# The last item's normalisation in the attention stage and in the scan stage, moved from GpSimd to ScalarE and VectorE

## The chip, the cores and the metric

The kernel runs on one core of a Trainium2 chip. The time is the device time of one launch in microseconds. A core has TensorE (matmuls, PE in the rows, PEld its weight loads), VectorE (DVE), ScalarE (ACT), GpSimd (POOL) and SyncE (SP), which here only asks for DMAs. Each engine runs a program of its own; they meet by semaphores.

## What is computed

Four layers of an attention part and a feed-forward part over x of 2048 rows of 256 numbers (8 items of 256 rows). The reference ends so, and each of the eight lines is a stage of the kernel:

```python
def _layernorm(x, axis=-1, eps=1e-05):
    m = jnp.mean(x, axis=axis, keepdims=True)
    v = jnp.var(x, axis=axis, keepdims=True)
    return (x - m) / jnp.sqrt(v + eps)
...
    x = _layernorm(x + _L1_attn_ref(x, ...), axis=-1)   # attention stage, l1_attn
    x = _layernorm(x + _L1_ffn_ref(x, ...), axis=-1)    # expert stage, l1_ffn
    x = _layernorm(x + _L2_attn_ref(x, ...), axis=-1)   # scan stage, l2_attn
    x = _layernorm(x + _L2_ffn_ref(x, ...), axis=-1)    # ternary stage, l2_ffn
```

The attention stage has 16 heads of 128. The expert stage routes each row to 4 of 32 experts. The scan stage is a selective scan with 16 states for each of 512 channels. The change concerns the last step of the attention stage and of the scan stage: for the last item, mean and variance of a row are known, and (x - m) / sqrt(v + eps) has to be written back.

## The kernel before

`program` (L4000) runs the stages one after the other. Each stage is a function that opens a `Block` in which it writes a program for each engine, and after it an `all_engine_barrier` (L4065) clears the stage's semaphores. X, the 8 items of x (128 rows x 2 x 256 each), stays in SBUF over all stages and is overwritten item by item.

At the end of a `Block` every engine executes a DRAIN, reports on a semaphore, and waits; GpSimd gathers the reports and releases the others. The barrier on L4065 does so a second time, with GpSimd clearing the semaphores between. The records of the first are put down to the line of the stage's `ExitStack`: L977 for the attention stage, L1444 for the expert stage, L1899 for the scan stage, L2586 for the ternary stage. A stage's first instructions follow the second.

The end of a stage for item i is made by helpers that all stages share. `add_and_stats` and `mean_and_variance` (L132 to L150): VectorE adds the residual into `r`, takes statistics of both halves of 128 rows, and aggregates them into `mv` (mean, variance), which raises `var_ready` by 1 for each half. `rstd` (L153): GpSimd waits for `var_ready`, adds `eps` into `vpe`, and takes it to the power of -0.5 into `rstd`. `normalize` (L161): VectorE waits for `rstd_ready` and writes X by a subtraction and a product for each half.

```python
def rstd(ph, pool, i):
    pool.wait_ge(ph.var_ready, (i + 1) * NT)
    ph.nc.gpsimd.tensor_tensor(ph.vpe[:, :], ph.mv[:, :, 1], ph.eps[:, :], ALU.add).then_inc(ph.eps_added, 1)
    pool.wait_ge(ph.eps_added, i + 1)
    ph.nc.gpsimd.tensor_tensor(ph.rstd[:, :], ph.vpe[:, :], ph.half[:, :], ALU.pow).then_inc(ph.rstd_ready, 1)
```

**Attention stage** (`l1_attn`, L968). The loop runs over 8 items and within them over 16 heads in a software pipeline of seven steps; the residual and the normalisation of item i - 1 stand inside item i. Beside it the kernel already routes the rows for the expert stage: GpSimd scatters the normalised rows of items 0 to 5 to memory, by indirect DMAs of 128 rows each, 8 for each item (`scatter`, L1404), two items late. After the last head VectorE takes the last item's residual and statistics, GpSimd its root (L1114), VectorE normalises (L1399), and nothing is left to overlap them with. SyncE asks for the experts' weights as the heads' weights are no longer needed, the last pieces when the last head's products are made.

**Expert stage** (`l1_ffn`, L1431). It begins with the transposes and the routing of the last item, the scatter of items 6 and 7, and the loads of sorted rows. GpSimd also asks here for the ternary stage's raw weights and stores them quantised (L1569, L1578).

**Scan stage** (`l2_attn`, L1878). GpSimd gathers the experts' results by 64 indirect DMAs (L2007), the last in item 4. In each item 16 scans run on VectorE; GpSimd multiplies each result by C (L2064), TensorE sums over the states. The normalisation is made another way here: GpSimd computes the root and also -mean * rstd (`pool_norm`, L2012, four operations, by `pool_rstd_out` for the stage's end), and ScalarE writes X with it as bias and scale (`act_out`, L2358). For the last item these stand at the end of GpSimd's and ScalarE's programs (L2084, L2441), behind the output product of the last item.

**Ternary stage** (`l2_ffn`, L2576). It loads its weights from memory after the barrier, turns them on TensorE, and then runs dense matmuls.

Of the kernel before, what the change touches and what calls it, by code (L numbers as in the profile page):

```python
# [20 lines left out]
ACT = mybir.ActivationFunctionType  # L21
AX_X = mybir.AxisListType.X

ITEMS, SEQ, D = 8, 256, 256
NT = SEQ // P
# [42 lines left out]
class Steps:  # L68
# [15 lines left out]
    def end(self):  # L84
        assert self.n == self.per_item, self.n
# [7 lines left out]
def stage(ph, pool, i):  # L93

    pool.wait_ge(ph.x_turned, i)
    ph.nc.gpsimd.tensor_copy(ph.xin[:, :, :], ph.X[:, i]).then_inc(ph.x_staged, 1)
# [56 lines left out]
def rstd(ph, pool, i):  # L153

    pool.wait_ge(ph.var_ready, (i + 1) * NT)
    ph.nc.gpsimd.tensor_tensor(ph.vpe[:, :], ph.mv[:, :, 1], ph.eps[:, :], ALU.add).then_inc(ph.eps_added, 1)  # L156
    pool.wait_ge(ph.eps_added, i + 1)
    ph.nc.gpsimd.tensor_tensor(ph.rstd[:, :], ph.vpe[:, :], ph.half[:, :], ALU.pow).then_inc(ph.rstd_ready, 1)


def normalize(ph, dve, i):  # L161

    dve.wait_ge(ph.rstd_ready, i + 1)
    for j in range(NT):
        ph.nc.vector.tensor_scalar(ph.X[:, i, j], ph.r[:, j, :], ph.mv[:, j, 0:1], ph.rstd[:, j:j + 1],  # L165
                                   ALU.subtract, ALU.mult).then_inc(ph.x_done, 1)
# [801 lines left out]
def l1_attn(nc, sh, w):  # L968
# [8 lines left out]
    with ExitStack() as ctx:  # L977
        ph = Phase(nc, ctx, "l1a", sh)
# [50 lines left out]
        def run(item, end):  # L1029

            def of(engine):
                item(0, 0, range(NH), first=True)
                item(1, 1, range(NH), second=True)
                for i in range(2, ITEMS):
                    item(i, i % 2, range(NH))
                end()
            return of
# [36 lines left out]
        @block.gpsimd  # L1074
        def _(pool):
            nc.gpsimd.memset(ones32[:, :], 1.0).then_inc(ones_ready, 1)
            pool.wait_ge(ones_ready, 1)
            nc.gpsimd.tensor_copy(ones[:, :], ones32[:, :]).then_inc(ones_ready, 1)
            stage(ph, pool, 0)
            nc.gpsimd.memset(routes.ones[:, :], 1.0).then_inc(consts_cleared, 1)  # L1080
            nc.gpsimd.memset(routes.lc[:, :, routes.E:], BIG).then_inc(consts_cleared, 1)
            nc.gpsimd.memset(routes.sel[:, :, :], 0.0).then_inc(consts_cleared, 1)
            nc.gpsimd.memset(routes.run[:, :, :], 0.0).then_inc(consts_cleared, 1)
            nc.gpsimd.memset(routes.base[:, :], 0.0).then_inc(consts_cleared, 1)
            nc.gpsimd.iota(room[:, :], [[routes.ROOM, routes.E]], base=0, channel_multiplier=0,
                           allow_small_or_imprecise_dtypes=True).then_inc(consts_cleared, 1)
            nc.gpsimd.memset(routes.ones_e[:, :], 1.0).then_inc(consts_cleared, 1)
            nc.gpsimd.iota(routes.full[:, :], [[P, ITEMS * NT]], base=P - 1, channel_multiplier=0,
                           allow_small_or_imprecise_dtypes=True).then_inc(consts_cleared, 1)
            nc.gpsimd.iota(routes.tau[:, :], [[0, 1]], base=0, channel_multiplier=1,  # L1090
                           allow_small_or_imprecise_dtypes=True).then_inc(consts_cleared, 1)
            pool.wait_ge(consts_cleared, 9)

            nc.gpsimd.affine_select(out=routes.tri[:, :], in_=routes.ones[:, :], compare_op=ALU.is_gt, fill=0.0,
                                    base=0, pattern=[[1, P]], channel_multiplier=-1).then_inc(consts_ready, 1)
            nc.gpsimd.tensor_copy(routes.base[0:1, :], room[0:1, :]).then_inc(consts_ready, 1)
            pool.wait_ge(consts_ready, 2)
            nc.gpsimd.memset(routes.base[32:33, :], 1.0).then_inc(consts_ready, 1)
            pool.wait_ge(consts_ready, 3)
            stage(ph, pool, 1)  # L1100
            for i in range(1, ITEMS):
                stage(ph, pool, i + 1)
                rstd(ph, pool, i - 1)
                pool.wait_ge(ph.x_done, i * NT)
                if i > 1:
                    pool.wait_ge(routing.turned, i - 1)
                nc.gpsimd.tensor_copy(xr, ph.X[:, i - 1]).then_inc(routing.x_ready, 1)
                if i == 2:
                    pool.wait_ge(sh.rows_cleared, 16)
                if i >= 2:  # L1110
                    pool.wait_ge(routing.idx_ready, i - 1)
                    for j in range(NT):
                        scatter(nc, pool, sh, i - 2, j, qk_ready, i * NH + 9 + j * routes.TOPK)
            rstd(ph, pool, ITEMS - 1)  # L1114

        @block.tensor
        def _(pe):
# [84 lines left out]
        def _(act):  # L1202
# [52 lines left out]
                        keep_high(ph, act, i + 1, xh[1 - p], YB[1 - p])  # L1255

            run(item, lambda: item(ITEMS - 1, 1, range(NH, NH + 6)))(act)

        @block.vector
        def _(dve):  # L1260
            keep_low(ph, dve, 0, xh[0], xl[0], xl_ready, YB[0])

            def residual(k, q):
                dve.wait_ge(ph.y_ready, k + 1)
                add_and_stats(ph, dve, k, YB[q][:, :].rearrange("p (j n) -> p j n", j=NT))
# [130 lines left out]
            def end():  # L1396
                item(ITEMS - 1, 1, range(NH, NH + 6))
                residual(ITEMS - 1, 1)
                normalize(ph, dve, ITEMS - 1)  # L1399

            run(item, end)(dve)

# [1 line left out]
def scatter(nc, pool, sh, i, j, pace=None, begun=0):  # L1404

    routes = sh.routes
    landed = routes.rows_out if i < ITEMS - 2 else routes.late_rows_out
    for k in range(routes.TOPK):
        if pace is not None:
            pool.wait_ge(pace, begun + k)  # L1410
        nc.gpsimd.indirect_dma_start(  # L1411
            out=sh.moe_rows, out_offset=bass.IndirectOffsetOnAxis(ap=routes.idx[:, i * NT + j, k:k + 1], axis=0),
            in_=sh.X[:, i, j, :], in_offset=None).then_inc(landed, 16)
# [464 lines left out]
def l2_attn(nc, sh, w):  # L1878
# [20 lines left out]
    with ExitStack() as ctx:  # L1899
        ph = Phase(nc, ctx, "l2a", sh)  # L1900
# [125 lines left out]
        def pool_rstd_out(pool, k):  # L2026
            pool_norm(pool, k, ph.var_ready, ph.eps_added, ph.rstd_ready, ph.x_done, shift_ready, ph.mv, ph.vpe, ph.rstd, r_sh)
# [6 lines left out]
        def _(pool):  # L2034
# [46 lines left out]

            for i in range(ITEMS):
                item(i, i % 2, first=i == 0, ahead=min(2, ITEMS - 1 - i))
            pool_rstd_out(pool, ITEMS - 1)  # L2084

        def pe_x(pe, k, q, pair):
            pe.wait_ge(ph.xT_ready, k + 1)
# [270 lines left out]
        def act_out(act, k):  # L2358
            act_norm(act, sh.X[:, k], ph.r, ph.rstd, r_sh, shift_ready, k, ph.x_done)

        @block.scalar
        def _(act):
# [75 lines left out]
                item(i, i % 2, first=i == 0, ahead=min(2, ITEMS - 1 - i))  # L2438
            for j in range(NT):
                act_keep_yg(act, ITEMS - 1, j)  # L2440
            act_out(act, ITEMS - 1)  # L2441

        def dve_conv(dve, k, pair):

# [72 lines left out]
        def _(dve):  # L2517
# [22 lines left out]
            def residual(k):  # L2540
                dve.wait_ge(ph.y_ready, k + 1)
                dve.wait_ge(ph.x_done, k * NT)
                add_and_stats(ph, dve, k, F[0][:, :].rearrange("p (j n) -> p j n", j=NT))
# [27 lines left out]
                item(i, i % 2, first=i == 0, ahead=min(2, ITEMS - 1 - i))  # L2571
            gate(ITEMS - 1, 1)
            residual(ITEMS - 1)


def l2_ffn(nc, sh, w):  # L2576
# [1522 lines left out]
```

## Time and profile before

| | us |
|---|---|
| runs, median (lowest to highest) of 3 | 2512.0 (2511.66 to 2514.43) |
| the profiled execution's own time | 2519.74 |
| its span, first to last instruction | 2518.0 |
| TensorE busy in it | 2217.8 (88%) |
| VectorE, ScalarE, GpSimd busy | 1674.2, 1453.1, 889.7 |
| mean granted clock of TensorE | 0.938 |

Times in rows are those of one profiled execution, counted from its span's start. An instruction of an engine counts as busy; a DRAIN, a semaphore instruction or a branch is the queue's own (written POOLq, DVEq) and does not. [...]

### The profile page before, as it was taken

Reading aid. Unit: us, or ns where it says so; the run is one execution under the profiler, and the core shown is the slowest. Engines: PE = TensorE matmul, PEld = TensorE weight load, DVE = VectorE, ACT = ScalarE, POOL = GpSimd, SP = SyncE. Lnnn points to the kernel's source line nnn. Section 1 sums busy time; section 2 is a strip of 40 time slices with the busy share of each in tenths; the row PEclk is TensorE's granted clock in tenths of the full one; section 3 lists DMA queues with packets and bytes.
Section 4 is the critical chain, followed back from the end, with each engine's and each line's share of the span. In section 5 each row is a group of like instructions: output and inputs, shape, how many; then the busy total and the mean of one; then the engine's idle time right before and its main releaser. Section 6 shows DMA issues by size and latency. Waiting matters only on the chain. (4 is left out here: it accounts for less than half of the span.)

```text
span 2518.0 us, 47690 instructions
## 1 busy us (share of the span) xinstructions
PE 2217.8 (88%) x16425; PEld 1937.2 (77%) x16425; DVE 1674.2 (66%) x4020; ACT 1453.1 (58%) x3815; POOL 889.7 (35%) x906
## 2 busy tenths in 40 slices
PE   6887979999999979998489999999686899996997
PEld 4776968999999959997266676677685576766997
DVE  5785767888888846554498898777464554554554
ACT  5674547777777723333487777775342566663342
POOL 3221240011111120000678887667485233332000
PEclk8897989999999979999699999999897999997999
DMA  4000120000000463333311111000400000000001
GB/s 151 1 1 17 35 68 18 2 18 18 18 18 18 144 197 119 120 111 94 129 41 51 51 50 47 35 35 1 119 1 1 1 1 1 1 1 1 1 1 34
DMA packets 74371, 111.77 MB, mean 44 GB/s; under 512 B 16174, under 2 KB 59814, under 8 KB 73016
## 3 DMA queue, kind: packets, MB, share of 16 engines
q1 hardware_dynamic: 66648, 87.23, 10.7%
q0 software_dynamic: 7488, 21.50, 2.6%
q8 instruction: 136, 2.23, 0.4%
q14 instruction: 99, 0.81, 0.1%
HBM read 79.73 MB, written 28.97 MB: 43 GB/s over the span
## 5 line engine op out<-in xcount | busy, mean ns | idle before, releaser
L2064 POOL TENSOR_TENSOR l2a_hb<-l2a_hb,l2a_Cb 128x1024 f32<-128x1024 f32 x128 | 302.8, 2377 | 107.7 <-DVE l2a_hb L2551 106.5
L2551 DVE TENSOR_TENSOR_SCAN l2a_hb<-l2a_dA,l2a_dB 128x1024 f32<-128x1024 f32 x128 | 288.8, 2275 | 31.4 <-PE l2a_dB L2158 26.1
L2158 PE MATMUL l2a_dB<-l2a_diag,l2a_dxT 64*128 64x128 f32 x2048 | 190.1, 306 | 38.8 <-DVE l2a_hb L2551 25.9
L2158 PEld LDWEIGHTS l2a_dB<-l2a_diag,l2a_dxT 64*128 64x128 f32 x2048 | 139.9, 194 | 104.0 <-PE l2a_dB L2158 37.2
L2388 ACT ACTIVATE l2a_dA<-l2a_delta,l2a_An 128x255 f32<-128x255 f32 x512 | 213.4, 498 | 6.9 <-DVE l2a_hb L2551 6.7
L964 PE MATMUL l1a_QK<-l1a_xh,early_wqkv_h 128*128 128x256 f32 x512 | 147.1, 287 | 1.5 <-DVE l1a_xl L128 1.5
L964 PE MATMUL l1a_QK<-l1a_xh,early_wqkv 128*128 128x256 f32 x512 | 144.6, 282 | 0.0
L964 PE MATMUL l1a_QK<-l1a_xl,early_wqkv_h 128*128 128x256 f32 x512 | 144.3, 282 | 0.0
L2178 PE MATMUL l2a_YS<-ident,l2a_hb 128*128 128x128 f32 x1024 | 142.2, 285 | 1.0 <-POOL l2a_hb L2064 1.0
L1240 ACT ACTIVATE l1a_ex<-l1a_S,l1a_nm 128x256 f32<-128x256 f32 x256 | 119.3, 471 | 36.5 <-DVE l1a_nm L1292 35.1
L2178 PEld LDWEIGHTS l2a_YS<-ident,l2a_hb 128*128 128x128 f32 x1024 | 116.5, 145 | 12.2 <-POOL l2a_hb L2064 1.3
L1275 DVE TENSOR_TENSOR l1a_qkl<-l1a_QK,l1a_qkh 128x512 fp32r<-128x512 f32 x128 | 88.0, 687 | 38.1 <-ACT l1a_qkh L1215 36.7
L3235 ACT COPY l3a_eT<-l3a_PT 128x512 f32<-128x512 f32 x96 | 56.8, 591 | 93.3 <-PE l3a_PT L3118 93.3
L1856 DVE TENSOR_TENSOR l1f_a<-l1f_s,l1f_GU 128x96 f32<-128x96 f32 x95 | 24.1, 254 | 128.5 <-ACT l1f_s L1680 128.5
L3369 DVE TENSOR_REDUCE l3a_mx<-l3a_S 128x2 f32<-128x512 f32 (+1 forms) x96 | 65.6, 684 | 63.6 <-PE l3a_S L3072 63.6
L3226 ACT ACTIVATE l3a_ex<-l3a_S,l3a_nm 128x128 f32<-128x128 f32 (+1 forms) x256 | 90.6, 435 | 22.1 <-DVE l3a_nm L3372 22.0
L1612 PE MATMUL l1f_GU<-routes_over_high,l1f_xt 128*128 x380 | 100.6, 389 | 0.0
L964 PEld LDWEIGHTS l1a_QK<-l1a_xh,early_wqkv_h 128*128 128x128 f32 x512 | 97.5, 190 | 1.9 <-issue 1.9
L156 POOL TENSOR_TENSOR l1a_vpe<-l1a_mv,eps 128x2 f32<-128x2 f32 x8 | 1.5, 193 | 275.3 <-DVE l1a_mv L150 275.3
L1411 POOL DMA_INDIRECT moe_x_rows<-X,routes_idx x64 | 64.0, 1000 | 96.9 <-PE l1a_QK L964 87.7
L964 PEld LDWEIGHTS l1a_QK<-l1a_xl,early_wqkv_h 128*128 128x128 f32 x512 | 97.4, 190 | 0.0
L964 PEld LDWEIGHTS l1a_QK<-l1a_xh,early_wqkv 128*128 128x128 f32 x512 | 97.3, 190 | 0.0
(767 smaller groups left out, 7812.4 us busy)
## 6 DMA issues: line engine op xcount, KB each, us to landing
l2a_Cb<-c_rows SPq DMA_DIRECT2D x8, 2048.0 KB
l1f_xl<-moe_x_rows SPq DMA_DIRECT2D x95, 128.0 KB
moe_y_rows<-l1f_yo SPq DMA_DIRECT2D x95, 128.0 KB, 1.7
first_raw<-in_L_attn_w_qkv_dram SPq DMA_DIRECT2D x18, 256.0 KB, 2.8
moe_x_rows<-X SPq DMA_DIRECT2D x1, 4224.0 KB, 17.2
l1f_dL<-in_L_ffn_Wd_dram SPq DMA_DIRECT2D x1, 3072.0 KB
X<-in_L_attn_x_dram SPq DMA_DIRECT2D x8, 256.0 KB, 6.0
routes_raw<-in_L_attn_w_o_dram SPq DMA_DIRECT2D x4, 512.0 KB
```

Of the source, the lines that this page charges most:

```text
L964: ins = pe.matmul(out, a, b, start=(first and n == 0), stop=(last and n == len(passes) - 1), **more)
L1240: last = nc.scalar.activation(ex[:, h % 2, j, :], S[h % 2][:, j * SEQ:(j + 1) * SEQ], ACT.Exp, bias=nm[:, h % 2, j:j + 1], scale=SCALE, ac ...
L1275: nc.vector.tensor_tensor(qkl[:, h % 2].rearrange("p n t -> p (n t)"), QK[h % 2][:, :], qkh[:, h % 2].rearrange("p n t -> p (n t)").bitcas ...
L1411: nc.gpsimd.indirect_dma_start(out=sh.moe_rows, out_offset=bass.IndirectOffsetOnAxis(ap=routes.idx[:, i * NT + j, k:k + 1], axis=0), in_=s ...
L1612: last = nc.tensor.matmul(GU[t % 2][:, 2 * EI:2 * (EI + SI)], xt[t % 2][:, kc, :], wS[:, kc, :, bass.ds(small, 1), :], start=(kc == 0), st ...
L2064: nc.gpsimd.tensor_tensor(h[:, :, :], h[:, :, :], Cb[p][:, s0:s0 + UN, :], ALU.mult).then_inc(hc_ready, 1)
L2158: last = nc.tensor.matmul(out[:, m:m + 2, j * P + a:j * P + a + HP], dxT[q][a:a + HP, j, c * P:(c + 1) * P], diag[q][a:a + HP, j, s0 + m:s ...
L2178: last = nc.tensor.matmul(YS[j][:, c * P:(c + 1) * P], hb[u % RING][:, n, j * P:(j + 1) * P], sh.ident[:, :], is_transpose=True, start=Fal ...
L2388: last = nc.scalar.activation(dA[(i * NU + u) % DAS][:, n, 1:SEQ], delta[q][:, c, 1:SEQ], ACT.Exp, scale=An[:, c, s0 + n:s0 + n + 1])
L2551: nc.vector.tensor_tensor_scan(flat(hb[u % RING]), flat(dA[(i * NU + u) % DAS]), dB[u % 2][:, :], 0.0, ALU.mult, ALU.add).then_inc(scanned, 1)
L3226: last = nc.scalar.activation(ex[:, b % NB, cols], S[b % 3][:, cols], ACT.Exp, bias=nm[:, b % NB, n:n + 1])
L3369: nc.vector.tensor_reduce(mx[:, b % NB, 0:nh], S[b % 3][:, :].rearrange("p (h k) -> p h k", h=nh), AX_X, ALU.max).then_inc(max_ready, 1)
```

## The change

Two helpers are added. `last_root` gives ScalarE a root of one column of `eps` into `vpe` (a value that is overwritten), and then, once the last item's variance is there, the root of variance + `eps` into `vpe`. `normalize_last` has VectorE take the reciprocal of that into `rstd` and call `normalize`. In the attention stage they take the place of GpSimd's `rstd` and of `normalize`. In the scan stage they take the place of GpSimd's `pool_rstd_out` and of ScalarE's `act_out` of the last item. All other items and stages keep their way. The root is now a table function of ScalarE and a reciprocal, where it was a power.

```diff
+def last_root(ph, act, per=1):
+    act.wait_ge(ph.rstd_ready, ITEMS - 1)
+    ph.nc.scalar.activation(ph.vpe[:, 0:1], ph.eps[:, 0:1], ACT.Sqrt).then_inc(ph.eps_added, 1)
+    act.wait_ge(ph.eps_added, (ITEMS - 1) * per + 1)
+    act.wait_ge(ph.var_ready, ITEMS * NT)
+    ph.nc.scalar.activation(ph.vpe[:, :], ph.mv[:, :, 1], ACT.Sqrt, bias=ph.eps[:, 0:1]).then_inc(ph.eps_added, 1)
+
+def normalize_last(ph, dve, per=1):
+    dve.wait_ge(ph.eps_added, (ITEMS - 1) * per + 2)
+    ph.nc.vector.reciprocal(ph.rstd[:, :], ph.vpe[:, :]).then_inc(ph.rstd_ready, 1)
+    normalize(ph, dve, ITEMS - 1)
...
 # l1_attn, GpSimd
-            rstd(ph, pool, ITEMS - 1)
 # l1_attn, ScalarE
             run(item, lambda: item(ITEMS - 1, 1, range(NH, NH + 6)))(act)
+            last_root(ph, act)
 # l1_attn, VectorE
                 residual(ITEMS - 1, 1)
-                normalize(ph, dve, ITEMS - 1)
+                normalize_last(ph, dve)
...
 # l2_attn, GpSimd
-            pool_rstd_out(pool, ITEMS - 1)
 # l2_attn, ScalarE
                 act_keep_yg(act, ITEMS - 1, j)
-            act_out(act, ITEMS - 1)
+            last_root(ph, act, 2)
 # l2_attn, VectorE
             residual(ITEMS - 1)
+            normalize_last(ph, dve, 2)
```

How the instructions stand. Line numbers behind the new helpers are 16 higher in the changed kernel. Semaphores have numbers that each stage uses anew, and the listing prints the first stage's name of a number: l0a_var_ready, l0a_eps_added, l0a_rstd_ready are this stage's `var_ready`, `eps_added`, `rstd_ready`.

GpSimd, end of the attention stage and begin of the expert stage, before:

```order
L1411 DMA moe_x_rows<-X,routes_idx 67584x256 [waits l0a_small_loaded] x7
L156 TENSOR_TENSOR l1a_vpe<-l1a_mv,eps 128x2 [waits l0a_var_ready]
L158 TENSOR_TENSOR l1a_rstd<-l1a_vpe,minus_half 128x2 [waits l0a_eps_added]
L977 UNCONDITIONAL_BRANCH
L4065 ISA [waits barrier_Pool_Activation_PE_DVE_SP_gather]
L1547 UNCONDITIONAL_BRANCH
```

and in the changed kernel:

```order
L1427 DMA moe_x_rows<-X,routes_idx 67584x256 [waits l0a_small_loaded] x7
L993 UNCONDITIONAL_BRANCH
L4081 ISA [waits barrier_Pool_Activation_PE_DVE_SP_gather]
L1563 UNCONDITIONAL_BRANCH
L1566 MEMSET l1f_a 128x256 x2
```

The last of the scatter's DMAs is now the last thing before the block's end (the branch, ahead of which the DRAIN stands).

ScalarE, end of the attention stage, in the changed kernel (before, the branch followed the last cast directly, and the table load for L1679 was there too):

```order
L1235 CAST l1a_vh<-l1a_val 128x256 [waits l0a_conv_ready]
L164 ACT_TABLE_LOAD
L164 ACTIVATE l1a_vpe<-eps 128x1 [waits l0a_rstd_ready]
L167 ACTIVATE l1a_vpe<-l1a_mv,eps 128x2 [waits l0a_var_ready,l0a_eps_added]
L993 UNCONDITIONAL_BRANCH
L1680 UNCONDITIONAL_BRANCH [waits barrier_Pool_Activation_PE_DVE_SP_release]
```

The load of the root's table stands ahead of the one-column root, with no wait of its own. ScalarE has three rows more in this stage and one more in the scan stage.

VectorE, end of the scan stage, in the changed kernel; before, the branch followed the aggregation:

```order
L146 BN_STATS l2a_stats<-l2a_r 128x6
L148 MEMSET l2a_carrier 128x1 [waits l0a_stats_ready]
L150 BN_AGGR l2a_mv<-l2a_stats 128x2 x2
L173 RECIPROCAL l2a_rstd<-l2a_vpe 128x2 [waits l0a_eps_added]
L181 TENSOR_SCALAR X<-l2a_r,l2a_mv,l2a_rstd 128x256 [waits l0a_rstd_ready]
L181 TENSOR_SCALAR X<-l2a_r,l2a_mv,l2a_rstd 128x256
```

VectorE's program of this stage now ends with three instructions more, and GpSimd's with four fewer, so that its last product with C (L2064) is its last work.

## Rows read from the trace of the kernel before

**Rows 1.** The page, busy time, share of the span and instructions of each engine.

```profile
PE 2217.8 (88%) x16425; PEld 1937.2 (77%) x16425; DVE 1674.2 (66%) x4020; ACT 1453.1 (58%) x3815; POOL 889.7 (35%) x906
```

**Rows 2.** Timeline, end of attention: start, us, engine, line, tiles [idle before <- releaser].

```profile
892.01 0.15 DVE L150 BATCH_NORM_AGGREGATE l1a_mv<-l1a_stats 128x2 f32<-128x6 f32 x1
892.52 0.72 POOL L158 TENSOR_TENSOR l1a_rstd<-l1a_vpe,minus_half 128x2 f32<-128x2 f32 x1
893.27 0.74 DVE L165 TENSOR_SCALAR X<-l1a_r,l1a_mv,l1a_rstd 128x256 f32<-128x256 f32 x2 [1.11 <-POOL l1a_rstd L158]
898.25 0.57 POOL L1550 MEMSET l1f_a<- 128x256 f32 x2 [5.01 <-POOLq L4065]
```

**Rows 3.** Queue instructions of L977, attention's block: ns min/median/max, first and last start.

```profile
L977 POOLq DRAIN  x1: 4767/4767/4767, 892.5 to 892.5; - x1
L977 DVEq DRAIN  x1: 771/771/771, 893.3 to 893.3; - x1
```

**Rows 4.** Timeline, end of the scan stage.

```profile
1774.26 0.15 DVE L150 BATCH_NORM_AGGREGATE l2a_mv<-l2a_stats 128x2 f32<-128x6 f32 x1
1775.74 0.20 POOL L2021 TENSOR_TENSOR l2a_r_sh<-l2a_r_sh,l2a_rstd 128x2 f32<-128x2 f32 x1
1775.97 1.09 ACT L2352 ACTIVATE X<-l2a_r,l2a_r_sh,l2a_rstd 128x256 f32<-128x256 f32 x2 [8.84 <-POOL l2a_r_sh L2021]
```

**Rows 5.** Queue instructions of L1899, the scan stage's block.

```profile
L1899 POOLq DRAIN  x1: 5543/5543/5543, 1775.7 to 1775.7; - x1
```

**Rows 6.** The same of L2586 (ternary stage) and L1444 (expert stage).

```profile
L2586 POOLq DRAIN  x1: 798/798/798, 1920.5 to 1920.5; - x1
...
L1444 POOLq DRAIN  x1: 2332/2332/2332, 1179.0 to 1179.0; - x1
```

**Rows 7.** GpSimd's DMAs by stage: attention (1), expert stage (4), scan stage (2).

```profile
L1411 POOL DMA_INDIRECT moe_x_rows<-X,routes_idx x48: 959/962/1271, 539.6 to 874.9; - x48
...
L1411 POOL DMA_INDIRECT moe_x_rows<-X,routes_idx x16: 960/963/1362, 899.3 to 918.8; - x16
...
L1569 POOL DMA_DIRECT2D routes_raw<-in_L_ffn_w_gate_up_dram x4: 751/775/832, 970.6 to 1012.7; - x4
L1569 POOL DMA_DIRECT2D routes_raw<-in_L_ffn_w_proj_dram x2: 537/543/549, 1046.5 to 1080.3; - x2
...
L1578 POOL DMA_DIRECT2D l2f_ternary<-l1f_hat x6: 542/554/564, 1007.0 to 1176.1; - x6
...
L2007 POOL DMA_INDIRECT l2a_my<-moe_y_rows,moe_back x48: 945/1000/1180, 1191.3 to 1534.8; - x48
L2007 POOL DMA_INDIRECT l2a_hb<-moe_y_rows,moe_back x16: 945/950/1101, 1201.8 to 1234.8; - x16
```

**Rows 8.** Timeline of GpSimd: its last work before the final normalisation, both stages.

```profile
874.91 0.96 POOL L1411 DMA_INDIRECT moe_x_rows<-X,routes_idx  x1 [3.72 <-PE l1a_QK L964]
...
1756.19 4.84 POOL L2064 TENSOR_TENSOR l2a_hb<-l2a_hb,l2a_Cb 128x1024 f32<-128x1024 f32 x2
```

**Rows 9.** ScalarE's last work in attention; lines L1679 (expert stage) and L1283 (attention).

```profile
888.48 0.40 ACT L1220 CAST l1a_vh<-l1a_val 128x256 fp32r<-128x256 f32 x1 [0.49 <-DVE l1a_val L1315]
...
L1679 ACT ACTIVATE l1f_s<-l1f_GU x95: 251/251/281, 912.2 to 1182.2; 128x96 f32<-128x96 f32 x95
L1679 ACT ACT_TABLE_LOAD  x2: 1283/1283/1283, 903.7 to 934.6; - x2
...
L1283 DVE RECIPROCAL l1a_rz<-l1a_z x128: 149/154/157, 386.1 to 883.1; 128x2 f32<-128x2 f32 x128
```

**Rows 10.** Timeline of VectorE while GpSimd's DRAIN of the expert stage runs.

```profile
1180.06 0.26 DVE L1856 TENSOR_TENSOR l1f_a<-l1f_s,l1f_GU 128x96 f32<-128x96 f32 x1 [2.03 <-ACT l1f_s L1680]
```

**Rows 11.** Stretches: us, busy us of each engine (instructions), granted clock, DMA share, GB/s.

```profile
896.00:897.00 1.00, 0.00 (x0) 0.00 (x0) 0.00 (x0) 0.00 (x0) 0.00 (x0) 0.50 0.41 97
...
1795.00:1798.00 3.00, 3.00 (x16) 3.00 (x16) 0.42 (x1) 0.46 (x2) 0.61 (x1) 0.50 0.66 115
1798.00:1812.00 14.00, 13.71 (x116) 13.53 (x115) 10.32 (x22) 8.06 (x24) 12.52 (x18) 1.00 0.66 184
```

## The prediction

> **What bounds the kernel now.** TensorE is busy for 88% of the span [rows 1], so I first looked for moments in which no engine works: the change sits at two of them. The stages are separated by barriers, and the views to read are the timeline around the two ends, and then the queues' own instructions on the stage's `Block` line, which are not counted as busy.
>
> In the attention stage VectorE's second aggregation ends at 892.16 us (892.01 + 0.15), GpSimd adds and takes the power until 893.24, and VectorE's two normalisations end at 894.01 [rows 2]. The expert stage's first instruction starts only at 898.25. The 4.2 us between are the thing to explain. The barrier's records tell: every engine executes a DRAIN before it reports. VectorE's ends at 893.3 + 0.77 = 894.07, right with its last work; GpSimd's starts at 892.5 and lasts 4.767 us, to 897.27 [rows 3]. So GpSimd is the last to arrive, 3.2 us after VectorE, although its own last work ended 4.03 us earlier.
>
> The scan stage repeats it. GpSimd's product ends at 1775.94, ScalarE's normalisation at 1777.06 [rows 4], and GpSimd's DRAIN, begun at 1775.7, lasts 5.543 us, to 1781.24 [rows 5].
>
> **What the long DRAIN is.** In the ternary stage GpSimd's DRAIN is 0.798 us, nearly all of it the power before it (0.72 us in [rows 2]); in the expert stage, where only semaphore waits stand before it, it is 2.332 us [rows 6]. The ternary stage issues no DMA from GpSimd. The others do: 48 in the attention stage, 16 + 6 + 6 = 28 in the expert stage, 48 + 16 = 64 in the scan stage [rows 7]. With the work that is still running taken off, the DRAINs are 4.03, 2.33 and 5.30 us: 84, 83 and 83 ns for each DMA. Three stages on one line through zero is a strong sign that the DRAIN pays for each DMA that GpSimd issued since the last barrier, however long ago it landed (the scan stage's last was issued at 1534.8). In the expert stage it ran from 1179.0 to 1181.3, while VectorE still worked [rows 6, 10]: it starts when GpSimd's program reaches it, and not when the others arrive. Whoever lets GpSimd arrive early hides it.
>
> **The change, part by part.** Attention stage. Removed: GpSimd's add and power after the last item. Its last work is then the scatter that ends at 874.91 + 0.96 = 875.87 [rows 8]; the DRAIN of 4.03 us ends at about 879.9, 13 us before anyone needs it. Cover: the last two heads' matmuls and splits.
> ScalarE gets a table load (1.283 us), a one-column root and the true root. Its last cast ends at 888.88 [rows 9]; the load ends at 890.17, the one-column root at 890.4, and 1.7 us of waiting remain until the variance: cost nothing. The wait has nothing behind it but the barrier. The load for the expert stage's Silu stood there before as well.
> On the path: a hand-over (0.03 to 0.09 between engines in [rows 2]; I take 0.05), the root, a hand-over, VectorE's reciprocal (0.154 [rows 9]), 0.05 to the next, and the same two normalisations (0.74). A root of 128x2 does not occur: below it is bounded by the reciprocal's 0.15, above by 0.28, the longest of the 128x96 activations [rows 9]; I take their usual 0.25, the nearest with a function and a table. Sum: 892.16 + 0.05 + 0.25 + 0.05 + 0.15 + 0.05 + 0.74 = 893.45; with 0.06 to VectorE's report, 893.51. Against 897.27 that is **3.76 us** earlier.
>
> Scan stage. Removed: four GpSimd operations and ScalarE's two normalisations. GpSimd's last product with C ends at 1756.19 + 4.84 = 1761.03 [rows 8], its 5.30 us of DRAIN at 1766.3, 8 us before the variance; the stage's output matmuls cover it. ScalarE idles from 1767.13 (1775.97 - 8.84 [rows 4]), so load and first root are done by 1768.7. The path from the variance at 1774.41 is the same 1.29 us + 0.06: 1775.76, against 1781.24: **5.48 us** earlier. VectorE's pair (0.74) replaces ScalarE's (1.09), inside that.
>
> Carried on. The next stage's first instructions come 0.98 us after the last report (897.27 to 898.25) and all its transfers are asked for after the barrier, so they move along, with one exception: the expert weights asked for at the end of attention. DMA still moves 97 GB/s in 896 to 897 us [rows 11]. The new expert stage starts near 894.5, its row loads about a microsecond later, so they queue behind these weights for up to some 1 us; the weights themselves have landed by about 897, 2.5 us into the new stage, and the transposes of the last item, its routing products and the row loads all come before their first use. I cost this at nothing and keep 1 us for the range.
>
> Sum: 3.76 + 5.48 = 9.2 us. The profiled execution took 2519.7 us, 7.7 above the median of 2512.0; from its own time I expect 2510.5, and from the median **2502.8 us**.
>
> [...] In the ternary stage a matmul costs 3.0/16 = 188 ns at the low level and 13.71/116 = 118 ns at the high one, so each microsecond of low clock more or less is worth 0.37 us. A shift of the low stretch by some 4 us is +-1.5 us: range.
>
> **Rivals.**
> (a) Forecast: both DRAINs hidden, all carried. 2502.8, with the bounds 2500 to 2505.5. For it: three stages on one line, and one of them already hidden. 70%.
> (b) The attention stage's part is lost. Either weights and routing hold the expert stage, or the early DRAIN hurts someone. At 876 to 880 VectorE is in the middle of heads with products of two SBUF operands; if GpSimd's DRAIN shut it out for its whole 4.0 us and TensorE could not make that up, the stage would gain nothing: 2512.0 - 5.5 = 2506.5. Against it: in the expert stage a product of 96 columns took 0.26 us inside the DRAIN [rows 10], which leaves no room for a stop, though it reads one operand from PSUM, so it proves little. [...] 11%.
> (c) The DRAIN is not what ends the barrier in an unprofiled run (the records themselves may stretch it; the profiled execution is 7.7 us above the median), or it does not move. Then only the root chain counts: 894.07 - 893.51 = 0.6 and 1777.06 + 0.06 - 1775.76 = 1.4 us: 2510.0. Against: nothing in the traces distinguishes it, and the DRAIN in the expert stage did move. 15%.
> (d) Slower: the shorter idle times change nothing in when the clock falls, but the earlier, thinner start of the ternary stage (transfers first, then bursts of transposes) lets the low level last into its dense matmuls. At 0.37 us for each microsecond it needs 25 us more of low clock to eat the 9.2 us, and 38 us (14 us lost) to be slower by over 5.0 us: 2517. Now the level is high throughout from 1798, 17 us after the barrier [rows 11]. 4%.
>
> **How the numbers follow.** About 0.2% or 5.0 us is what a measurement of this kernel can tell from no change. (a) is faster by 9.2, nearly (b) only by 5.5, so half of (b) is counted as faster; (c) is within; (d) slower. Faster 0.70 + 0.06 = 0.76, and 0.02 more for a mixture of (a) and (c): 0.78; same 0.18; slower 0.04. The time is (a)'s. Range: (a)'s bounds (root and hand-overs +-0.3 at each end, queueing 1, clock 1.5) and (b)'s 2506.5 with one microsecond: 2499.8 to 2508.0 holds 81%.
>
> **What would show it.** Right: on the `Block` lines GpSimd's DRAIN begins near 876 and 1761 with 4.0 and 5.3 us, VectorE's is the last to end, near 893.5 and (with the first gain) 1772.0; the table load stands right behind ScalarE's last copy; idle time between the last normalisation and the next stage's first instruction is 1.0 us at both ends, where it is 4.2 us at the first now. Wrong: a DRAIN that still ends last; VectorE's two-operand products longer than before while it runs; the root waiting for its table; or the gain at 1778 us visible and gone by the ternary stage's end.

## The result, and the profile after

| | before | after |
|---|---|---|
| median of the first comparison (4 executions each) | 2511.84 us | 2498.36 us |
| lowest to highest | 2511.66 to 2514.43 | 2497.57 to 2501.90 |
| the profiled execution, its span | 2519.74, 2518.0 | 2501.90, 2500.2 |
| granted clock in it | 0.938 | 0.942 |

The granted clock is TensorE's, as a share of its full speed: 1.00 or 0.50 in every record of the 14 profiled executions, and a value between in a stretch that holds both.

The ratio is 0.9947, with a 95% interval of 0.9929 to 0.9964: the kernel became 13.5 us faster by the medians. 9.2 us were forecast, and the time lies 1.4 us below the lower end of the range. Of the 33 executions of the kernel before that served as reference on the chip of the first four experiments, one took 5167 us, a slow run that no ratio counts. In the changed kernel the lines after the two new helpers have numbers 16 higher: the attention stage's block is L993, the scan stage's L1915.

The end of the attention stage, in the timeline of the changed kernel (answering to [rows 2]; the columns are those of [rows 2]):

```profile
882.53 1.28 ACT L164 ACT_TABLE_LOAD   x1
...
883.82 0.20 ACT L164 ACTIVATE l1a_vpe<-eps 128x1 f32<-128x1 f32 x1
...
885.64 0.15 DVE L150 BATCH_NORM_AGGREGATE l1a_mv<-l1a_stats 128x2 f32<-128x6 f32 x1
885.88 0.29 ACT L167 ACTIVATE l1a_vpe<-l1a_mv,eps 128x2 f32<-128x2 f32 x1 [1.86 <-DVE l1a_mv L150]
886.21 0.17 DVE L173 RECIPROCAL l1a_rstd<-l1a_vpe 128x2 f32<-128x2 f32 x1 [0.42 <-ACT l1a_vpe L167]
886.41 0.74 DVE L181 TENSOR_SCALAR X<-l1a_r,l1a_mv,l1a_rstd 128x256 f32<-128x256 f32 x2
888.23 0.57 POOL L1566 MEMSET l1f_a<- 128x256 f32 x2 [18.71 <-POOLq L4081]
```

From the end of the second aggregation (885.79) to the end of the normalisations (887.15) are 1.36 us, where [rows 2] had 1.85. Then 1.08 us pass until the next stage's first instruction, where [rows 2] had 4.24. ScalarE's table load and first root are over at 884.02, 1.77 us before the variance (885.79).

The queues' own instructions on the two block lines (answering to [rows 3] and [rows 5]; nanoseconds as min/median/max, then first and last start):

```profile
L993 POOLq DRAIN  x1: 8240/8240/8240, 868.3 to 868.3; - x1
L993 PEldq DRAIN  x1: 1005/1005/1005, 883.0 to 883.0; - x1
...
L993 ACTq DRAIN  x1: 306/306/306, 885.9 to 885.9; - x1
L993 DVEq DRAIN  x1: 771/771/771, 886.4 to 886.4; - x1
```

```profile
L1915 POOLq DRAIN  x1: 8617/8617/8617, 1744.8 to 1744.8; - x1
L1915 PEldq DRAIN  x1: 5257/5257/5257, 1754.5 to 1754.5; - x1
L1915 ACTq DRAIN  x1: 308/308/308, 1761.6 to 1761.6; - x1
L1915 DVEq DRAIN  x1: 771/771/771, 1762.1 to 1762.1; - x1
```

Both barriers are now ended by VectorE, at 887.2 and 1762.9. GpSimd's DRAINs end at 876.6 and 1753.4, 10.6 and 9.5 us earlier, beside other work. Measured at the place, from the end of the second aggregation to the barrier's release (the start of GpSimd's first instruction on the barrier's line), the attention stage's end took 5.30 us before and 1.60 now, and the scan stage's 7.04 before and 1.61 now: 3.70 + 5.43 = **9.1 us**, against 3.76 + 5.48 = 9.2 forecast. Below, "from the variance to the release" is this measure.

So the question that is left is where the other 4 us came from. Stage by stage, from barrier to barrier (us; the first stage is l0_attn, the last two are l3_attn and l3_ffn), the two profiled executions differ in stages that the change does not touch:

```
stage          before    after
first          246.34   240.03    same code in both
l0_ffn         125.62   125.63    same code
attention      525.49   521.74    -3.75
expert         292.33   290.24    same code
scan           591.66   585.46    -6.20
ternary        140.77   140.33    same code
last two       587.05   588.01    same code
```

The first stage runs before anything that the change touches, and is 6.3 us shorter. The stretches of one item in it, in the kernel before and in the changed one (us, busy time of PE, PEld, DVE, ACT and POOL with their instructions, granted clock, DMA share, GB/s):

```profile
197.50:224.80 27.30, 24.59 (x154) 21.78 (x153) 20.05 (x59) 16.24 (x45) 5.25 (x6) 0.81 0.00 1
```

```profile
194.10:218.50 24.40, 20.34 (x152) 17.88 (x152) 19.07 (x58) 16.25 (x45) 5.25 (x6) 0.99 0.00 1
```

Nearly the same matmuls in both, ScalarE and GpSimd equally busy, and TensorE's granted clock is 0.81 in the one and 0.99 in the other: a part of the item, 214.2 to 221.0 us above all, had a granted clock of 0.50. The items of this stage, the first and the last apart, take from 24.3 to 27.3 us in the traces, in no fixed order.

### The profile page after: what moved, and what is told of

Read it like the earlier page. It is cut to its first block and busy times, and to the rows that moved or that the text cites. A ratio compares the mean times of both kernels' runs of the same rounds, so it can differ in the third digit from the quotient of the medians.

```text
span 2500.2 us, 47670 instructions
## 1 busy us (share of the span) xinstructions
PE 2205.6 (88%) x16402; PEld 1930.6 (77%) x16425; DVE 1672.5 (67%) x4024; ACT 1456.0 (58%) x3819; POOL 887.2 (35%) x900
## 5 line engine op out<-in xcount | busy, mean ns | idle before, releaser
L1247 ACT ACTIVATE l1a_pr<-l1a_ex,l1a_rz 128x256 f32<-128x256 f32 x128 | 65.3, 510 | 52.3 <-DVE l1a_rz L1299 49.6
```

The lines of the kernel that those rows point to most:

```text
L1247: nc.scalar.activation(pr0[:, h % 2, :], ex[:, h % 2, 0, :], ACT.Copy, scale=rz[:, h % 2, 0:1]).then_inc(probs_ready, 1)
```

## The experiments

Two theories had to be told apart from their rivals. **The DRAIN**: it costs about 83 ns for each DMA that GpSimd issued since its last one, and starts when GpSimd reaches it. **The spread**: the change is worth its two ends, about 9 to 10 us, and the rest of 13.5 belongs to that one comparison and not to the change. Each comparison below has its own reference runs of the kernel before, on the chip where it was made.

**The attention part alone.** GpSimd's last root, ScalarE's normalisation and the rest of the scan stage as before:

```diff
 (changed kernel, scan stage)
+            pool_rstd_out(pool, ITEMS - 1)
-            last_root(ph, act, 2)
+            act_out(act, ITEMS - 1)
-            normalize_last(ph, dve, 2)
```

> The change in the attention stage alone. Theory (GpSimd's DRAIN pays about 83 ns for each DMA issued since the last barrier, starts when GpSimd's program ends, and the expert stage gains more than it is given because its first tiles start before the down weights are asked for): attention stage 3.8 us shorter, expert stage 2.0 us shorter, scan stage unchanged: 5.8 us faster than before, 2506.0. Rival 1 (the expert stage's 2.0 us in the two profiled runs was chance): 3.8 us, 2508.0, and an expert stage of 292.3 us as before. Rival 2 (the DRAIN costs time only in a profiled run): 0.6 us, 2511.2.

Measured: ratio 0.9992 (0.9984 to 1.0001), medians 2507.35 against 2509.11. In its profile the attention stage takes 521.76 us (3.7 less), the scan stage 590.99, and the expert stage 289.99.

**The scan part alone.** The other half:

```diff
 (changed kernel, attention stage)
+            rstd(ph, pool, ITEMS - 1)
-            last_root(ph, act)
-                normalize_last(ph, dve)
+                normalize(ph, dve, ITEMS - 1)
```

> The change in the scan stage alone. Theory: scan stage 5.5 to 6.3 us shorter, the others as before: 2505.5 to 2506.3. If the gain of the whole change (13.4) is the sum of its parts, this run and the attention part alone give 13.4 together, and the 1.9 us that the stage lengths of the two profiled runs do not show must lie in one of them. Rival (DRAIN only in a profiled run): 1.4 us, 2510.4.

Measured: ratio 0.9985 (0.9976 to 0.9993), medians 2504.71 against 2509.11. The scan stage takes 585.35 us, the attention stage 525.47 as before, and the expert stage 289.85, although its start was not moved. That settles the expert stage: its 2 us had nothing to do with the earlier start. Over all profiled executions it takes 289.9 to 292.6 us with either start. The two parts gave 1.8 + 4.4 us by the medians of these comparisons, less than their ends give in the traces (3.7 + 5.4) and far less than 13.5; the intervals of both (up to 4.0 and 6.0 us) still hold what the traces say. The first four experiments share their reference runs, and each gained 1 to 3 us less than was forecast for its ends (1.8 for 3.8, 4.4 for 5.5, -0.5 for 1.4 and 4.3 for 7.3); why, no run shows.

**The DRAIN late again.**

```diff
 (changed kernel, end of GpSimd's program in both stages)
+            pool.wait_ge(ph.rstd_ready, ITEMS)
```

> The whole change, but GpSimd waits for the last reciprocal before it leaves its program in both stages, without doing anything. Theory (the DRAIN is what was taken off the path): GpSimd arrives last again; from variance to barrier 0.05+0.25+0.05+0.15+0.05+4.03 = 4.6 us in the attention stage (5.1 before, 1.3 with the change) and 5.9 us in the scan stage (6.8 before). So only 0.5 + 0.9 = 1.4 us of the gain stay: 2510.4, and the expert stage goes back to 292.3 us if its gain comes from the earlier start. Rival (root chain and profiling effect): the DRAIN does not matter in an unprofiled run, 2498.4 as with the change.

Measured: ratio 1.0001 (0.9992 to 1.0010), medians 2509.63 against 2509.11. One wait that does nothing takes the gain away, in runs without a profile too; the interval (up to 2.0 us faster) still holds the 1.4 us that were forecast to stay. Queue instructions of the two blocks (L993 and, a line further down, L1916):

```profile
L993 DVEq DRAIN  x1: 771/771/771, 890.8 to 890.8; - x1
L993 POOLq DRAIN  x1: 3978/3978/3978, 890.9 to 890.9; - x1
```

```profile
L1916 DVEq DRAIN  x1: 769/769/769, 1769.0 to 1769.0; - x1
L1916 POOLq DRAIN  x1: 5277/5277/5277, 1769.2 to 1769.2; - x1
```

With nothing else running on GpSimd the two lengths are clean: 3978/48 = 82.9 ns and 5277/64 = 82.5 ns for each DMA. The root chain is the changed kernel's here. From the variance to the release the two ends take 4.97 and 6.28 us, where they took 5.30 and 7.04: the shorter chain is worth 0.33 + 0.76 = 1.1 us by itself, of 9.1.

**The DRAIN early, and nothing else.** The kernel before, with root and normalisations where they were:

```diff
 (kernel before, both stages, ahead of rstd and pool_rstd_out of the last item)
+            nc.gpsimd.drain()
```

> The kernel before, root and last normalisation where they were, with one explicit DRAIN on GpSimd ahead of the last item's add and power, in both stages. Theory (the DRAIN pays once for each DMA since the DRAIN before it): the explicit one takes 4 to 7 us beside other work, the one at the barrier falls to under 0.1 us plus the power that still runs (0.80 us as in the ternary stage). Attention stage: barrier at VectorE's last normalisation, 894.07 for 897.27: 3.2 us; scan stage: at ScalarE's, 1777.1 for 1781.24: 4.1 us; with the expert stage's 2.0 that is 9.3 us: 2502.5. Rival 1 (the DRAIN's length is fixed by what the stage issued and is paid at every DRAIN): two long DRAINs and no gain, 2511.8. Rival 2 (profiling effect): 2511.8, with a short DRAIN in the profile.

Measured: ratio 0.9979 (0.9969 to 0.9988), medians 2504.78 against 2509.11. The added DRAINs, L1114 and L2085, and those at the two barriers:

```profile
L1114 POOLq DRAIN  x1: 8192/8192/8192, 872.8 to 872.8; - x1
```

```profile
L2085 POOLq DRAIN  x1: 8603/8603/8603, 1752.5 to 1752.5; - x1
```

```profile
L977 POOLq DRAIN  x1: 821/821/821, 890.6 to 890.6; - x1
L977 DVEq DRAIN  x1: 773/773/773, 891.4 to 891.4; - x1
```

```profile
L1900 POOLq DRAIN  x1: 305/305/305, 1770.5 to 1770.5; - x1
L1900 ACTq DRAIN  x1: 1121/1121/1121, 1770.7 to 1770.7; - x1
```

What was 4.77 and 5.54 us is 0.82 and 0.31: the cost is paid once, at whichever DRAIN comes first. From the variance to the release the ends take 2.09 and 2.88 us: 3.2 + 4.2 = 7.4 us less than before, against 7.3 forecast for them. The stages are 3.1 and 3.8 us shorter (522.35 and 587.88 us). The 2.0 us that the forecast added for the expert stage did not come, and the medians show 4.3 us (3.0 to 7.8 by the interval). By the traces one line in each stage, without moving any work, has most of the gain; by the medians it has about half.

**More DMAs where there were none.** The stages of [rows 6] and [rows 7] could fit one line by chance, so 32 small DMAs were added in each of two stages that issue none:

```diff
 (kernel before, l3_attn; in l3_ffn one row: scratch[4 * i + n, 0:1, :], sh.half[0:1, :])
+                for n in range(4):
+                    nc.gpsimd.dma_start(scratch[4 * i + n, :, :], sh.half[:, :]).then_inc(extra_out, 16)
...
+            pool.wait_ge(extra_out, 16 * 32)
             rstd(ph, pool, ITEMS - 1)
```

> The kernel before, with 32 small DMAs more issued by GpSimd in each of the last two stages, which issue none: 128 rows of 8 bytes each in l3_attn, one row of 8 bytes in l3_ffn, all landed before the last item's root. Theory (83 ns for each DMA, whatever its size): both DRAINs grow from 0.79 to 0.79 + 32 x 0.083 = 3.45 us, GpSimd becomes the last at both barriers, 1.9 us later each: 3.9 us slower. Rival 1 (the cost goes with rows or bytes): l3_ffn's DRAIN stays at 0.79 us and l3_attn's grows by another amount than l3_ffn's. Rival 2 (the length belongs to indirect DMAs or to these stages): both DRAINs stay at 0.79 us, no change of the time.

Measured: ratio 1.0017 (1.0002 to 1.0031), medians 2517.81 against 2512.38. Queue instructions of l3_attn's block (L2835) and l3_ffn's (L3415):

```profile
L2835 POOLq DRAIN  x1: 3424/3424/3424, 2301.1 to 2301.1; - x1
L2835 DVEq DRAIN  x1: 771/771/771, 2301.9 to 2301.9; - x1
```

```profile
L3415 POOLq DRAIN  x1: 3446/3446/3446, 2507.2 to 2507.2; - x1
L3415 DVEq DRAIN  x1: 769/769/769, 2508.0 to 2508.0; - x1
```

Both were 0.79 us in the kernel before, and 3.45 was expected: (3.42 - 0.79)/32 = 82 ns and (3.45 - 0.79)/32 = 83 ns. With 128 rows or one, and direct instead of indirect (82.9 and 82.5 ns in the late DRAINs), each DMA costs the same within 1 ns, and the last of the added DMAs had landed 25 and 11 us before. VectorE's report stands 2.09 us ahead of the barrier's release instead of 0.20, and from the variance to the release the ends take 4.01 and 4.04 us for 2.06: 3.9 us lost, as forecast, of the 5.4 between the medians.

**The DRAIN after its last DMA has landed.** The early DRAIN of the attention stage was forecast at 4.0 us and took 8.2:

```diff
 (changed kernel, end of GpSimd's program in the attention stage)
+            pool.wait_ge(routes.rows_out, 16 * (ITEMS - 2) * NT * routes.TOPK)
```

> The changed kernel, with one wait of GpSimd ahead of the end of its attention program: for the landing of its scatters. It tells what the early DRAIN spends beyond 48 x 83 ns (8.24 us instead of 4.0, from the moment that its last scatter is issued). Theory (the DRAIN first lets the last scatter land, 4.2 us after its issue, and then pays for each): the DRAIN begins about 4 us later, lasts 4.0 us and ends at the same time. Rival (beside running transfers and VectorE's work each of the 48 costs twice as much): it begins 4 us later and still lasts 7 us. No time lost either way.

```profile
L993 POOLq DRAIN  x1: 3978/3978/3978, 878.0 to 878.0; - x1
```

It takes 3.98 us again, though the DMA engines (share 1.00 from 878 to 882) and VectorE work beside it, so the rival (each of the 48 costs twice as much beside other work) is refuted. The theory fits only in part. The last scatter was issued at 872.15 in this run, and the DRAIN ends at 882.0, 9.9 us later; in the changed kernel it was issued at 868.56 and the DRAIN ended at 876.56, 8.0 us later. If the DRAIN only waited for the landing and then paid for each, both would end at the same distance. The landings say more: in the changed kernel the last scatter lands at 874.56, and the DRAIN ends 2.00 us after it. In the three other traces of an early DRAIN that have this landing it is 2.00 or 2.01 us as well (875.63 to 877.64, 878.95 to 880.96, 880.47 to 882.47). In none of them does an early DRAIN end before the last DMA has landed, and by an estimate from 2.00 and 3.98 about half of its cost is spent by then. What it does in detail beside the transfer stays open; it lies hidden in either case (the profiled execution, the only one, took 2502.4 us).

**The spread.** The kernel before against itself, and the changed kernel three times more, each beside its own reference runs:

> The kernel before against itself, to see the spread. Expected: a ratio of 1 and a median within 1.5 us of the reference runs. In its profile: attention stage 525.4 us, expert stage anywhere from 289.9 to 292.5, scan stage 591.0 to 591.7. Theory (the first stage's length is a matter of the execution): it may come out at 240 as well as at 244. Rival (the first stage is shorter in the kernels in which GpSimd leaves the attention stage early: 239.1 to 241.0 us in four of them, 243.2 to 246.3 in the five others): over 243.

Measured: ratio 1.0003 (0.9993 to 1.0014), medians 2512.88 against 2512.80; single executions from 2507.4 to 2520.4. Its first stage took 241.0 us, under the 243 that the rival wanted; its scan stage took 592.8, 1.1 us more than was expected.

> The changed kernel once more, in more executions than the first time and beside the kernel before on the same chip. Theory (the change is worth 3.75 us in the attention stage and 5.9 us in the scan stage, and the rest of the 13.4 us was the spread of the other stages between executions: 2.0 us in the expert stage and 6.3 us in the first stage between the two profiled runs, where the two kernels are the same): about 9.6 us faster, 2499.5 against 2509.1. Rival (the change gives 13.4 us in every comparison, through something later that the parts alone did not trigger): 2495.7.

> The changed kernel for the third time. Theory (stages: 3.7 + 5.4 = 9.1 us, everything else spread): 9.1 +- 2 us faster. Rival (13.4 is the change's own, with the first stage's 4 us in it): 13.4. In its profile the first stage at 239 to 241 us speaks for the rival, over 243 against it.

> The changed kernel for the fourth time, since its three comparisons gave 13.4, 7.8 and 10.5 us. Theory (attention 3.7 + scan 5.7 = 9.4 us, the rest is spread of the other stages): 9.4 +- 2 us faster. Rival (4 us more than the two ends give are the change's own): 13.4. In the profile: attention stage 521.7 to 521.9, scan stage 583.7 to 587.0.

```
changed kernel   ratio   95% interval       medians            gain   executions
first            0.9947  0.9929 to 0.9964   2498.4 / 2511.8    13.5    4
second           0.9968  0.9953 to 0.9983   2504.6 / 2512.4     7.8   10
third            0.9957  0.9942 to 0.9972   2502.3 / 2512.8    10.5    6
fourth           0.9966  0.9954 to 0.9979   2501.5 / 2509.3     7.8    7
```

The three later comparisons, weighted by their executions, give 8.5 us, and all four 9.3. In the third one's profile the first stage took 241.7 us, between the marks that were set. In the fourth one's it took 246.0 us, as long as in the kernel before, and the span was still 2499.8: the rival that ties the first stage to the change is refuted. The same stages over the 14 profiled executions (the late and the early DRAIN, whose ends are neither the one nor the other, stand only in the rows of all):

```
attention, root on GpSimd             525.36 to 525.50   (4 traces)
attention, as in the changed kernel   521.73 to 521.90   (6 traces)
  the same behind the shorter l0_ffn  521.30             (2 traces, last experiment)
scan, as before                       590.99 to 592.80   (4 traces)
scan, as in the changed kernel        583.67 to 587.75   (8 traces)
first stage, all                      239.1  to 246.3
expert stage, all                     289.9  to 292.6
ternary stage, all                    137.7  to 141.0
l3_attn, no DMAs added                380.8  to 384.8

from the variance to the release      attention          scan stage
  as before                           5.29 to 5.30 (4)   7.04 to 7.05 (4 traces)
  as in the changed kernel            1.60 to 1.61 (8)   1.60 to 1.61 (8 traces)
```

The two ends repeat to 0.01 us in every trace, so the 9.1 us are sharp. The attention stage as a whole repeats to 0.2 us. The scan stage varies by up to 4.1 us with the same code; its mean fell by 5.8 us, of which 5.4 are seen at its end and the remaining 0.4 are within its spread.

**The same at the other ends.** A version that should beat both: the two helpers also in l0_ffn, the ternary stage and the last two.

```diff
 (changed kernel, l0_ffn)
-            rstd(ph, pool, ITEMS - 1)
-            normalize_here(ITEMS - 1)
...
+            last_root(ph, act)
...
+            normalize_last(ph, dve)
 (ternary stage, l3_attn, l3_ffn: likewise for rstd and normalize)
```

> The changed kernel, and the same two helpers also at the end of the first expert-free stage after the first one (l0_ffn), of the ternary stage and of the last two stages. Theory: in l0_ffn GpSimd adds, takes the power and normalises (0.20 + 0.71 + 2.42 us) and reaches the barrier at 365.45, 3.66 us after the variance; 1.29 + 0.06 us instead: 2.3 us. In the three others GpSimd's DRAIN ends 0.75 us before VectorE's and issues no DMA to pay for: only the root chain, 0.56 us each, as the attention stage showed between variance and last normalisation (1.85 to 1.29): 1.7 us. Sum 4.0 us faster than the changed kernel in the same comparison. Rival (the table load that Sqrt needs delays a Silu or Exp of the next stage, where the activation before it had its table already): 1.28 us back at each of four ends, a gain near nothing.

> The version with the two helpers at six ends once more, with more executions. Theory: 4.0 us faster than the changed kernel in the same comparison (2.3 in l0_ffn, 0.56 at each of three ends), 13.1 us faster than before. Rival (the 5.9 us between the two medians of the first comparison are its own): 6 us faster than the changed kernel.

Measured: ratios to the kernel before of 0.9940 (0.9922 to 0.9957) and 0.9952 (0.9939 to 0.9964), medians 13.7 and 11.8 us faster than before; against the changed kernel in the same two comparisons 5.9 and 1.3 us faster. l0_ffn takes 123.3 and 123.5 us, where all others took 125.0 to 126.4. Its end in the first of the two:

```profile
362.44 0.15 DVE L150 BATCH_NORM_AGGREGATE l0f_mv<-l0f_stats 128x2 f32<-128x6 f32 x1
362.68 0.29 ACT L167 ACTIVATE l0f_vpe<-l0f_mv,eps 128x2 f32<-128x2 f32 x1 [8.47 <-DVE l0f_mv L150]
363.01 0.17 DVE L173 RECIPROCAL l0f_rstd<-l0f_vpe 128x2 f32<-128x2 f32 x1 [0.42 <-ACT l0f_vpe L167]
363.21 0.73 DVE L181 TENSOR_SCALAR X<-l0f_r,l0f_mv,l0f_rstd 128x256 f32<-128x256 f32 x2
```

From the variance to the release l0_ffn's end takes 1.60 us in both traces, where it took 3.88: the 2.3 us that were forecast. The three other ends take 1.60 or 1.61, where they took 2.06: 0.45 us each for the 0.56 forecast. The sum is 3.6 us for 4.0. The rival was a table load more in each next stage: ScalarE has 104 loads in the first of these traces and 98 in the kernel before, and the six more all stand on L164, so the next stages load no more than they did. The version is faster than before in both comparisons; the sum fits the two gaps to the changed kernel (5.9 and 1.3), but the intervals overlap, and 12 executions do not show it by themselves.

## Why the prediction was wrong

**The DRAIN** was right, point by point: per DMA and not per byte (82 and 83 ns each for 128 rows and for one), once per DMA (8.19 us at the added DRAIN, 0.82 at the barrier behind it), started by GpSimd's own program (at 868.3 us, where it was 892.5), and paid in unprofiled runs too (with the late DRAIN the ratio is 1.0001). Rival (c), only the root chain, is refuted by the late DRAIN (no gain beyond the noise, and 1.1 us at the ends, with the whole chain in place) and by the early one (a gain with none of it).

**The sum of the two ends** was right: 3.70 and 5.43 us measured against 3.76 and 5.48, and the same in every later trace. The root took 0.29 and 0.30 us where I took 0.25, the three hand-overs 0.09, 0.04 and 0.03 where I took 0.05 each, the reciprocal 0.17 for 0.15.

**The early DRAIN's length** was wrong in the attention stage, 8.2 us for 4.0, and cost nothing, since 13 us of cover were forecast there. The prediction let the DRAIN begin behind the last scatter and had no term for a scatter that has not landed; the DRAIN ended 2.00 us after its landing. In the scan stage it took 8.6 from 1744.8 because GpSimd's last product ran under it until 1748.1; the 5.3 us behind that are the forecast ones. Rival (b), VectorE shut out meanwhile, is refuted. In the changed kernel's timeline, inside the DRAIN of 868.3 to 876.6:

```profile
870.73 0.42 DVE L1317 TENSOR_TENSOR l1a_prl<-l1a_pr,l1a_prh 128x256 fp32r<-128x256 f32 x1
871.06 0.48 DVE L1324 SCALAR_TENSOR_TENSOR l1a_pr<-l1a_ex,l1a_rz,l1a_pr 128x256 f32<-128x256 f32 x1
```

The same two operations in the run that waited for the landing, inside its DRAIN of 878.0 to 882.0:

```profile
880.77 0.42 DVE L1318 TENSOR_TENSOR l1a_prl<-l1a_pr,l1a_prh 128x256 fp32r<-128x256 f32 x1
881.11 0.48 DVE L1325 SCALAR_TENSOR_TENSOR l1a_pr<-l1a_ex,l1a_rz,l1a_pr 128x256 f32<-128x256 f32 x1
```

Inside both DRAINs VectorE's operations on two SBUF operands keep their 0.42 and 0.48 us, which are their medians over the stage in the kernel before (418 and 478 ns).

**"Carried on"**, costed at nothing with 1 us for the range, held. The expert stage is not longer for its earlier start, and the 2 us by which it looked shorter come without the change as well. Rival (d) did not happen.

**The clock's 1.5 us** in the range rest on a low stretch moved by some 4 us, and no run shows this term. In the two profiled executions of the first comparison the granted clock fell to 0.50 at 893.4 before and at 887.2 with the change, 3.1 and 3.2 us after the end of the attention stage's last matmul (890.36 and 883.99), and behind the scan stage's last one 4.9 and 4.7 us after its end (1772.61 and 1759.69). In the 40 us from that fall on it was 0.50 for 27.3 us behind the attention stage in both traces of the kernel before, and for 20.5 us in all four of the changed kernel; behind the scan stage for 17.1 us in both, and for 17.1, 6.8, 6.8 and 6.8 us. The expert stage took 292.3 and 291.3 us before and 290.1 to 292.1 with the change, the ternary stage 140.8 and 139.2 us, and 137.8 to 140.3: by their lengths the effect is not told from the spread.

**The step that failed is the range.** I wrote "(a)'s bounds (root and hand-overs +-0.3 at each end, queueing 1, clock 1.5)" and so gave the unknown costs of the change, and nothing for how far one comparison of a few executions strays. That term it put at nothing without a reason. The runs showed that the same two kernels compare at 13.5, 7.8, 10.5 and 7.8 us, and that between executions of the same code the first stage moves by 7.3 us, the expert stage by 2.8, the scan stage by up to 4.1, the ternary stage by 3.3 and l3_attn by 4.1. In three of these the length mostly goes with TensorE's granted clock: the first stage took 246.3 and 246.0 us at 0.86 and 0.87, and 241.0 at 0.89; the ternary stage 141.0 at 0.91 and 137.7 at 0.95; l3_attn 384.8 at 0.95 and 380.8 at 0.96. In the expert stage (292.1 and 290.1 us, both at 0.96) and the scan stage as before (592.8 us at 0.92, 591.0 at 0.91) it does not.

The sign of it stood in the first table: a profiled execution 7.7 us above a median whose three runs agreed to 2.8. The point forecast of 9.2 us lies inside the intervals of all four comparisons (the first one's 0.9964 is 9.0 us), and the measured 13.5 is one draw. That the same two kernels later came to 7.8, 10.5 and 7.8 says that the other 4 us are not the change's. What they were stays open.

The mean granted clock of an execution does not tell: in the four executions of the changed kernel in the first comparison it was 0.942, 0.945, 0.945 and 0.946, 0.9445 in the mean, and 0.9442 in the 23 later ones, which took 2503.0 us in the mean where those four took 2499.1. That the forecast mechanism was right is shown; that the range missed by 1.4 us is the luck of one comparison that it had not allowed for, and the three later medians (2504.6, 2502.3 and 2501.5) lie inside it.

## What to carry to other kernels

Where GpSimd issues DMAs, look for its DRAIN at the next barrier: here it was 83 ns for each of them, paid once, from the moment its program ended. Let GpSimd finish early, or give it a DRAIN of its own in a stretch where nobody waits for it; move its last short operation to another engine only if the chain itself is worth something.

Compare kernels by stage before believing a difference of a few us: a stage with the same code that differs between two traces gives the spread for nothing, and a range must contain it. Where a change is meant to shorten a stage's end, measure that end: here it repeated to 0.01 us, where the stages around it moved by 3 to 7 us.

## What the runs showed of the hardware that I had not expected

- In the stages measured the DRAIN's cost went by the number of DMAs alone: 82 to 83 ns for indirect ones of 128 rows, for the expert stage's mix with 12 direct ones, and for direct ones of 128 rows or of one row of 8 bytes.
- ScalarE's table load took 1.28 us and the root stood right behind it (882.53 + 1.28 = 883.81, the root at 883.82), issued as soon as the last cast was done, ahead of the wait for the variance.
- An early DRAIN over a DMA still in flight was longer (8.2 us) than one that waited for the landing first (3.98), but ended sooner, 8.0 instead of 9.9 us after the issue. It ended 2.00 to 2.01 us after the landing in all four traces that show the landing.
